# Eight experts for every row, or two: rows scattered into expert order by indirect transfers

## The chip, the cores and the metric

The kernel runs on one core of one Trainium2 chip. The metric is device time in microseconds (us), one launch. A core has TensorE (PE: matrix products into PSUM), VectorE (DVE), ScalarE (ACT), GpSimd (POOL), which can't read PSUM, and SyncE (SP), which issues transfers between the core's SBUF and the chip's memory (DRAM). The engines run their own instruction lists in order and meet at semaphores.

## The reference

A two-layer network over 16 sequences of 256 rows of 128 numbers, 4096 rows in all. Each layer adds (attention) x silu(gated part) to its input. The gated part of the first layer is a mixture of experts, and only its arithmetic matters here:

```
scores = softmax(x @ gate_w.T)                # 8 experts
topw, topi = top_k(scores, 2); topw /= sum(topw)
eo[e]  = (silu(x @ wg[e]) * (x @ wu[e])) @ wd[e]      # each 128 -> 176 -> 128
y      = sum over the two chosen experts of topw * eo
shared = (silu(x @ swg) * (x @ swu)) @ swd            # 128 -> 352 -> 128
g      = silu(y + shared);  x = x + attention * g
```

The reference computes all eight eo for every row and weighs six of them by zero. All numbers are fp32.

## The kernel before

`build_kernel` runs stages one after another, each in a block of its own with a barrier behind it: `front` (layer norm, router logits, loads), `window_attention`, `experts`, then `normalise`, `bias_attention` and `inner_layers` for the second layer. Rows stand in 32 tiles of 128 (X: the running sum, Y: the normalised rows, S: the attention's result).

`window_attention` goes through 64 units (half the heads of a tile at a time; four units make a batch of two tiles). A unit is: scores on PE (L601), a table added and the row maximum on DVE (L701, L705), the maximum taken off on POOL (`shift`, L552), exp on ACT (L676), eight transposes on PE (L609), a copy on ACT (L681), products with the values on PE (L629, L633). POOL also masks the keys of each batch (L546). PE works units off in order; DVE works four units ahead, with six buffers. PSUM bank 7 serves all other small products, in a written order of jobs (JOBS), one at a time. Between units DVE runs `choose_experts` in six parts (two largest of eight scores by maximum and comparison, their weights, and the weights split into three bf16 parts, `wparts`).

`experts` holds all weights side by side as 1760 columns: 1408 routed (8 x 176) and 352 shared, 14 chunks. Each fp32 product is made of three products of rounded and remaining parts (`split_product`, L1118 to L1120). For each of 8 rounds of 512 rows and each chunk, PE makes the gate and the up half (6 products), spreads the rows' weights over the chunk's columns with a 0/1 matrix (L1149), and takes the chunk of two steps before through the down weights (3 products) into one PSUM bank. ACT takes silu and the rounded part (L1208, L1221), DVE multiplies twice (L1258, L1262), POOL makes the remaining part (L1237). A row's weight multiplies its hidden values, so unchosen experts add zero. After 14 chunks ACT takes silu of the sum, PE transposes it, DVE multiplies by S and adds to X (L1265, L1268) and takes statistics (L1272).

```
split_product(ps[0:n, s % 2, :], (wgu_hi[:, 0, a:a + n], wgu_lo[:, 0, a:a + n]), here).then_inc(gate_ps, 1)
...
nc.tensor.matmul(ps[:, 4 + s % 2, :], sel16[:, a:a + n], wT[:, parity, :], start=True, stop=True).then_inc(route_ps, 1)
```

Of the kernel before, what the change touches and what calls it, by code (L numbers as in the profile page):

```python
# [28 lines left out]
RSQRT_MAGIC = 1597463007.0  # L29

# [16 lines left out]
def shape_constants():  # L47
# [19 lines left out]
    select = np.zeros((NE, ROUTED), np.float32)  # L67
    select[np.arange(ROUTED) // INTER, np.arange(ROUTED)] = 1.0
# [6 lines left out]
        "c_select": np.tile(select, (3, 1)),  # L75
# [5 lines left out]
def build_kernel(nc, t, out):  # L81
    ctx = ExitStack()
    with ctx:
# [7 lines left out]
        with ExitStack() as early:  # L91
            S = early.enter_context(nc.sbuf_tensor("S0", [P, NT, P], F32))
            wparts = early.enter_context(nc.sbuf_tensor("wparts", [P, NT, 3 * NE], F32))
            wgu = early.enter_context(nc.sbuf_tensor("wgu", [P, 2, FEAT], F32))
            wd = early.enter_context(nc.sbuf_tensor("wd", [P, len(chunks(FEAT)), P], F32))
            sel = early.enter_context(nc.sbuf_tensor("sel", [3 * NE, ROUTED], F32))
            experts_loaded = early.enter_context(nc.semaphore("experts_loaded"))

            with ExitStack() as first:
# [4 lines left out]
                front(nc, t, ps, X, Y, ident, wgu, wd, sel, experts_loaded, skew, attn, route)  # L104
                window_attention(nc, "a0", t, ps, ident, Y, S, attn, lambda dve, part: choose_experts(nc, dve, part, route, wparts))
            experts(nc, t, ps, ident, X, Y, S, wparts, (wgu, wd, sel, experts_loaded), stats)
# [125 lines left out]

def router_buffers(nc, ctx):

    sb = lambda n, s, d=F32: ctx.enter_context(nc.sbuf_tensor("r_" + n, s, d))
    wide = {n: sb(n, [P, NT, NE]) for n in ("lg", "rest", "first", "second", "wdense")}
    return {**wide, "desc": sb("desc", [P, NE]), "st": sb("st", [P, NT]), "rounded": sb("rounded", [P, NT, NE], BF16)}


def choose_experts(nc, dve, part, route, wparts):  # L240

    lg, rest, first, second, wdense, desc, st, rounded = (route[n] for n in (
        "lg", "rest", "first", "second", "wdense", "desc", "st", "rounded"))
# [3 lines left out]
    def first_of_largest(dst, src):  # L247

        nc.vector.tensor_reduce(st[:, :], src, AX.X, ALU.max)
        dve.drain()  # L250
        nc.vector.tensor_tensor(dst, src, bc(st), ALU.is_equal)
# [8 lines left out]
    if part == 0:  # L260
# [6 lines left out]
        first_of_largest(first[:], lg[:])  # L267
        nc.vector.scalar_tensor_tensor(rest[:], first[:], -2.0, lg[:], ALU.mult, ALU.add)
        dve.drain()
    elif part == 1:  # L270
        first_of_largest(second[:], rest[:])
        nc.vector.tensor_tensor(first[:], first[:], second[:], ALU.add)
        dve.drain()
    elif part == 2:
        nc.vector.tensor_tensor(wdense[:], lg[:], first[:], ALU.mult)
        dve.drain()
        nc.vector.tensor_reduce(st[:, :], wdense[:], AX.X, ALU.add)
# [5 lines left out]
        nc.vector.tensor_tensor(wdense[:], wdense[:], bc(st), ALU.mult)  # L283
        dve.drain()
    else:
        v = part - 3
        kept = wparts[:, :, NE * v:NE * (v + 1)]
        nc.vector.tensor_copy(rounded[:], wdense[:])
        dve.drain()
        nc.vector.tensor_copy(kept, rounded[:])  # L290
        dve.drain()
        if v < 2:
            nc.vector.tensor_tensor(wdense[:], wdense[:], kept, ALU.subtract)
            dve.drain()


def front(nc, t, ps, X, Y, ident, wgu, wd, sel, experts_loaded, skew, attn, route):

    NR, full = ROUTED // P, SHARED // P
    ROUNDS = NT // 4  # L300
    QT = NT // 4
    with ExitStack() as c:
        sb = lambda n, s, d=F32: c.enter_context(nc.sbuf_tensor("r_" + n, s, d))
        sem = lambda n: c.enter_context(nc.semaphore("r_" + n))
# [1867 lines left out]
```

## Time and profile before

| | before |
|---|---|
| runs | 1708.53 us median of 3 (1708.19 to 1713.43) |
| profiled execution | span 1708.8 us, from the first to the last instruction |
| window attention | 30 to 261.6 us |
| experts | 261.6 to 560.0 us |
| PE, DVE, ACT, POOL busy over the span | 89%, 77%, 71%, 64% |

The profile gives one execution. An engine is busy while it runs an instruction; semaphore and register instructions and the issuing of transfers are not counted. A fp32 product of PE shows as two MATMUL records, one of rounded operands and a transpose as one; records overlap, since the engine is pipelined, so the distance between starts says more than a record's length. The granted clock of PE is a share of 2.4 GHz.

### The profile page before, as it was taken

The numbers are of one execution on the slowest core, as the hardware profiler recorded it, in microseconds if no ns is written. First come the engines' busy times: TensorE is split into PE (matmuls) and PEld (weight loads), VectorE is DVE, ScalarE is ACT, GpSimd is POOL, SyncE is SP. The second block draws the span as 40 slices with busy tenths as digits, with TensorE's granted clock in tenths as the row PEclk, the third lists the DMA queues.
The fourth block names the chain that finished last, engine by engine and source line by source line (L and its number), as shares of the span: only waits on it lengthen the run. The fifth ranks groups of instructions, "written<-read, shape, count | busy, mean of one in ns | idle before, by whom it ended". The sixth has DMA issues, their size and how long they took to land. (4 is left out here: it accounts for less than half of the span.)

```text
span 1708.8 us, 44008 instructions
## 1 busy us (share of the span) xinstructions
PE 1513.5 (89%) x16988; PEld 1164.6 (68%) x16988; DVE 1319.0 (77%) x2187; ACT 1217.6 (71%) x2065; POOL 1099.4 (64%) x661
## 2 busy tenths in 40 slices
PE   5899996999999499999999578899999999999885
PEld 4677774677776266666666467777777777777774
DVE  5899974555655699999997788887888888888753
ACT  2677774545445488888888378888888888888873
POOL 1777752555555388888887477776676777667614
PEclk8899998999999699999999689999999999999997
DMA  5000000000000500000000001111111110111113
GB/s 174 2 3 3 3 3 15 15 8 7 7 7 1 185 2 2 14 2 14 2 14 11 13 22 31 27 26 27 27 27 27 27 26 22 26 27 27 27 27 105
DMA packets 56837, 44.12 MB, mean 26 GB/s; under 512 B 28152, under 2 KB 47900, under 8 KB 56388
## 3 DMA queue, kind: packets, MB, share of 16 engines
q1 hardware_dynamic: 56644, 41.45, 9.1%
q8 instruction: 133, 2.18, 0.5%
q14 instruction: 60, 0.49, 0.1%
HBM read 17.75 MB, written 4.23 MB: 13 GB/s over the span
## 5 line engine op out<-in xcount | busy, mean ns | idle before, releaser
L831 POOL TENSOR_TENSOR a_prob<-a_prob,a_top 128x1024 f32<-128x1024 f32 x128 | 239.8, 1895 | 48.2 <-DVE a_top L1023 48.2
L1237 POOL TENSOR_TENSOR e_hh<-e_h,e_hh 128x512 fp32r<-128x512 f32 x112 | 144.8, 1293 | 146.6 <-ACT e_hh L1221 145.2
L1506 POOL TENSOR_TENSOR i_qk<-i_qk,i_rt 128x1024 f32<-128x1024 f32 x64 | 152.0, 2375 | 38.1 <-DVE i_rt L1955 33.3
L1516 POOL TENSOR_TENSOR i_qk<-i_qk,i_rn 128x1024 f32<-128x1024 f32 x64 | 122.5, 1915 | 80.5 <-DVE i_rn L1934 80.5
L1019 DVE TENSOR_TENSOR a_prob<-ps,a_table 128x1024 f32<-128x1024 f32 x128 | 149.7, 1211 | 23.4 <-PE ps L899 21.3
L1811 ACT ACTIVATE i_prob<-i_prob,i_top 128x128 f32<-128x128 f32 x512 | 156.4, 391 | 15.7 <-DVE i_top L1943 13.8
L977 ACT ACTIVATE a_probT<-ps 128x1024 f32<-128x1024 f32 x128 | 131.3, 1026 | 44.5 <-PE ps L907 44.5
L1258 DVE TENSOR_TENSOR e_h<-ps,e_sg 128x512 f32<-128x512 f32 x112 | 77.3, 690 | 104.3 <-PE ps L1120 90.4
L907 PEld LDWEIGHTS ps<-ident,a_prob 128*128 128x128 f32 x1024 | 113.2, 141 | 64.2 <-ACT a_probT L977 50.3
L1503 POOL TENSOR_TENSOR i_qk<-i_raw,i_rot 128x1024 f32<-128x1024 f32 x59 | 140.3, 2378 | 24.1 <-issue 24.1
L1208 ACT ACTIVATE e_sg<-ps 128x512 f32<-128x512 f32 x112 | 67.0, 598 | 123.2 <-PE ps L1120 122.4
L1023 DVE TENSOR_REDUCE a_top<-a_prob 128x4 f32<-128x1024 f32 x128 | 149.5, 1209 | 0.0
L907 PE MATMUL ps<-ident,a_prob 128*128 128x128 f32 x1024 | 138.6, 279 | 5.9 <-ACT a_probT L977 1.3
L552 POOL TENSOR_TENSOR a_prob<-a_prob,a_top 128x1024 f32<-128x1024 f32 x64 | 120.2, 1899 | 28.5 <-DVE a_top L705 28.5
L972 ACT ACTIVATE a_prob<-a_prob 128x1024 f32<-128x1024 f32 x128 | 135.4, 1058 | 0.6 <-POOL a_prob L831 0.6
L1776 ACT ACTIVATE i_raw<-ps 128x1024 f32<-128x1024 f32 x64 | 65.6, 1025 | 76.9 <-PE ps L1573 76.7
L1118 PE MATMUL ps<-e_xT,e_wgu_hi 128*128 128x512 f32 x224 | 89.6, 400 | 4.7 <-DVE e_wd_lo L1284 4.7
L1120 PE MATMUL ps<-e_xT,e_wgu_lo 128*128 128x512 f32 x224 | 89.0, 397 | 0.0
L1119 PE MATMUL ps<-e_xT,e_wgu_hi 128*128 128x512 f32 x224 | 88.7, 396 | 0.0
L1652 PE MATMUL ps<-i_wo,i_oT 128*128 128x128 f32 x512 | 71.8, 285 | 18.6 <-ACT i_oT L1822 18.6
L1955 DVE TENSOR_TENSOR i_rt<-ps,i_rot 128x512 f32<-128x512 f32 x128 | 82.0, 682 | 6.0 <-ACT i_raw L1776 6.0
L1652 PEld LDWEIGHTS ps<-i_wo,i_oT 128*128 128x128 f32 x512 | 65.0, 198 | 28.2 <-ACT i_oT L1822 18.7
(305 smaller groups left out, 4369.3 us busy)
## 6 DMA issues: line engine op xcount, KB each, us to landing
i_V<-i_V SPq DMA_DIRECT2D x96, 130.0 KB, 2.3
a_table<-skew_scratch SPq DMA_DIRECT2D x2, 2048.0 KB, 12.4
X<-in_L_attn_x SPq DMA_DIRECT2D x4, 512.0 KB, 6.1
a_table<-in_c_l_table SPq DMA_DIRECT2D x1, 2048.0 KB, 8.3
e_xs<-Y SPq DMA_DIRECT2D x8, 256.0 KB, 2.3
i_ms<-Y SPq DMA_DIRECT2D x16, 128.0 KB, 2.4
i_ms<-Y SPq DMA_DIRECT2D x16, 112.0 KB, 2.4
out_dram<-X SPq DMA_DIRECT2D x7, 256.0 KB, 2.3
```

What stands on the lines that cost most here:

```text
L831: nc.gpsimd.tensor_tensor(s, s, top[:, slot].unsqueeze(2).broadcast_to([P, HG, KW]), ALU.subtract).then_inc(shifted, 1)
L907: last = nc.tensor.transpose(ps[:, 4 + b // 4, b % 4 * P:(b % 4 + 1) * P], flat[:, b * P:(b + 1) * P], ident[:, :])
L972: nc.scalar.activation(s, s, ACT.Exp).then_inc(exped, 1)
L977: nc.scalar.activation(probT[:, n % 4].rearrange('p (b n) -> p b n', b=2), ps[:, 4:6, :], ACT.Copy).then_inc(pT_sb, 1)
L1019: nc.vector.tensor_tensor(prob[:, slot].rearrange('p (b x) k -> p b x k', b=2), ps[:, 2 * (n % 2):2 * (n % 2) + 2, :].rearrange('p b (x k) ...
L1023: nc.vector.tensor_reduce(top[:, slot], prob[:, slot], AX.X, ALU.max).then_inc(max_done, 1)
L1237: nc.gpsimd.tensor_tensor(hh[0:n, slot(b, parity), 1, :], h[0:n, slot(b, parity), :], hh[0:n, slot(b, parity), 0, :].bitcast(F32), ALU.sub ...
L1503: nc.gpsimd.tensor_tensor(s, raw[:, T % 2], cosines, ALU.mult).then_inc(cos_done, 1)
L1506: nc.gpsimd.tensor_tensor(s, s, rt[:], ALU.add).then_inc(rotated, 1)
L1516: nc.gpsimd.tensor_tensor(flat, flat, rn[:, T // TPB % 2, T % TPB].unsqueeze(2).broadcast_to([P, 2 * FH, FD]), ALU.mult).then_inc(qk_done, 1)
L1652: last = nc.tensor.matmul(ps[:, 3, 0:P], oT[:, u, :], wo[:, layer(T), u, :], start=(u == 0), stop=(u == 3))
L1811: last = nc.scalar.activation(s, s, ACT.Exp, bias=top[:, T % 2, h:h + 1])
```

## The change

`front` loads the routed weights by expert (`wr`, `wd`) and the shared ones apart (`wsh`, `wds`). `choose_experts` keeps each row's two weights and computes where it goes: in each expert's own run of rows, padded to whole blocks of 128 (72 blocks hold 8192 chosen rows and the padding). PE counts with two products (the job `ranks`), DVE adds up the counts. From unit 21 of `window_attention` on, POOL writes the rows into that order in DRAM by 64 indirect transfers (`scatter`: 128 rows of 512 bytes, each to the place in `slot`), two behind each `shift`; SP has written zeros there before. `experts` then has two halves. In the first, 36 pairs of blocks are read back, transposed, taken through one expert's weights, which PE addresses by a number that it loads into a register (`value_load`, 24 at a time), and stored to DRAM (`results`). In the second, the shared expert runs as before, 3 chunks and 8 rounds, while POOL gathers each row's two results by 64 indirect transfers (`fetch`), in between its subtractions (`low`); DVE adds them by weight (`mix`), ACT takes silu, DVE updates X (`renew`).

```diff
 def choose_experts(nc, dve, part, route, place, ranks, ranks_ready, ranks_taken):
...
+        nc.vector.tensor_tensor(rest[:], first[:], second[:], ALU.add).then_inc(route["chosen"], 1)
...
+    elif part == 3:
+        totals, before = ranks[:, 0:NE * NT], ranks[:, NE * NT:2 * NE * NT]
+        dve.wait_ge(*ranks_ready)
+        nc.vector.tensor_tensor_scan(incl[:, :], rank[:, P:P + NE * NT], totals, 0.0, ALU.mult, ALU.add)
...
+    elif part == 4:
...
+            nc.vector.tensor_copy(place["slot"][c][:, :], st[:, :]).then_inc(place["ranked"], 1)
...
+            sp.dma_start(route["rank"][:, :], t["c_rank"]).then_inc(gate_loaded, 16)
...
+            nc.gpsimd.memset(wd[:, :, 1, :], 0.0).then_inc(wd_cleared, 1)
+            nc.gpsimd.memset(route["ones"][:, :], 1.0)
...
 def window_attention(nc, name, t, ps, ident, Y, S, attn, route, place, spent):
...
+    RANKS = 11
+    SCATTERS, PER_UNIT = RANKS + 10, 2
...
+        PARTS = {2: 1, 4: 2, RANKS + 1: 3, RANKS + 3: 4, RANKS + 5: 5}
...
+            sp.wait_ge(zeroed, NZERO)
+            for q in range(NBLOCKS // 4):
+                rows = place["sorted"][4 * P * q:4 * P * (q + 1), :].rearrange("(k p) e -> p k e", p=P)
+                sp.dma_start(rows, place["zeros"][:]).then_inc(place["cleared"], 16)
...
+            nc.gpsimd.memset(place["zeros"][:], 0.0).then_inc(zeroed, 1)
...
+            nc.clear_and_free_semaphores(spent)
+
+            def scatter(r):
+                c, T = divmod(r, NT)
+                if T == 0:
+                    pool.wait_ge(place["ranked"], c + 1)
+                    pool.wait_ge(place["cleared"], 16 * (NBLOCKS // 4))
+                nc.gpsimd.indirect_dma_start(place["sorted"], bass.IndirectOffsetOnAxis(ap=place["slot"][c][:, T:T + 1], axis=0),
+                                             Y[:, T, :], None).then_inc(place["scattered"], 16)
+
             mask_keys(0)
             for n in range(UNITS):
...
                 shift(n)
-                i, r = divmod(n + 2, U)
+                for r in range(PER_UNIT * (n - SCATTERS), PER_UNIT * (n - SCATTERS + 1)):
+                    if 0 <= r < 2 * NT:
+                        scatter(r)
...
+                elif kind == 'ranks':
+                    pe.wait_ge(route["chosen"], 1)
+                    both = route["rest"][:].rearrange("p t e -> p e t")
+                    nc.tensor.matmul(ps[:, 7, 0:NE * NT], route["ones"][:, :], both, start=True, stop=True)
+                    last = nc.tensor.matmul(ps[:, 7, NE * NT:2 * NE * NT], route["rank"][:, 0:P], both, start=True, stop=True)
...
-                if step >= 4 and step % 8 == 4 and step // 8 < 5:
-                    between(dve, 1 + step // 8)
+                if step in PARTS:
+                    choose(PARTS[step])
...
+def experts(nc, t, ps, ident, X, Y, S, place, weights, stats):
...
+            sp.wait_ge(place["scattered"], 16 * 2 * NT)
+            for q in range(QUADS):
+                stage(q)
+                if q >= XBUF - 1:
+                    keep(q - XBUF + 1)
...
+        @block.gpsimd
+        def _(pool):
+            def fetch(i):
+                after(pool, mixed, i - RBUF + 1)
+                for k in range(4):
+                    for ch in range(2):
+                        nc.gpsimd.indirect_dma_start(back[:, i % RBUF, ch, k, :], None, place["results"],
+                                                     bass.IndirectOffsetOnAxis(ap=place["slot"][ch][:, 4 * i + k:4 * i + k + 1], axis=0)).then_inc(returned[i % RBUF], 16)
...
+            for q in range(2):
+                pool.wait_ge(kept[q], 16 * QUADS // 2)
+            fetch(0)
+            for i in range(ROUNDS):
+                if i + 1 < ROUNDS and i + 1 < RBUF:
+                    fetch(i + 1)
+                for s in range(NC):
+                    low(i * NC + s)
+                if RBUF <= i + 1 < ROUNDS:
+                    fetch(i + 1)
...
+            def into(j, owners):
+                pe.wait_ge(rowsT_sb, j // 2 + 1)
+                after(pe, hid_sb, j - 1)
+                for k in range(2):
+                    at = (2 * j + k) % 4 * P
+                    last = nc.tensor.matmul(ps[:, 2 * (j % 2) + k, 0:PAIR], rowsT[:, j // 2 % 2, at:at + P],
+                                            wr[:, bass.ds(owners[k], 1), :, :].rearrange("p a j i -> p (a j i)"), start=True, stop=True)
+                last.then_inc(pair_ps, 1)
...
+            def load_owners(a):
+                for b in range(a, min(a + LOADED, NBLOCKS)):
+                    owners[b] = pe.value_load(place["owner"][0:1, b:b + 1], min_val=0, max_val=NE - 1)
+
+            transpose_rows(0)
+            for j in range(PAIRS + 2):
+                if 2 * j % LOADED == 0 and j < PAIRS:
+                    load_owners(2 * j)
+                if j < PAIRS:
+                    into(j, [owners[2 * j + k] for k in range(2)])
+                if j % 2 == 0 and j // 2 + 1 < QUADS:
+                    transpose_rows(j // 2 + 1)
+                if 0 <= j - 1 < PAIRS:
+                    transpose_hidden(j - 1)
+                if 0 <= j - 2 < PAIRS:
+                    back_out(j - 2, [owners[2 * (j - 2) + k] for k in range(2)])
...
+            def mix(i):
+                dve.wait_ge(out_T, i + 1)
+                dve.wait_ge(returned[i % RBUF], 16 * 8 * (i // RBUF + 1))
...
+                if s == 2 and 0 <= i - 1 < ROUNDS:
+                    mix(i - 1)
+                if s == 1 and 0 <= i - 2 < ROUNDS:
+                    renew(i - 2)
+            renew(ROUNDS - 1)
```

## Rows read from the trace of the kernel before

**Rows 1.** Page, part 1: busy us of each engine (share of the span) xinstructions
```profile
PE 1513.5 (89%) x16988; PEld 1164.6 (68%) x16988; DVE 1319.0 (77%) x2187; ACT 1217.6 (71%) x2065; POOL 1099.4 (64%) x661
```

**Rows 2.** Busy time by stretch: us, busy us (xrecords) of each engine, clock, DMA share, GB/s
```profile
82.00:261.60 179.60, 174.68 (x3812) 130.47 (x3810) 158.06 (x174) 134.09 (x213) 119.90 (x64) 1.00 0.01 3
261.60:276.30 14.70, 2.23 (x8) 1.43 (x8) 6.42 (x4) 8.44 (x7) 1.73 (x2) 0.56 0.15 42
276.30:556.00 279.70, 272.16 (x1180) 197.86 (x1180) 157.04 (x249) 138.67 (x245) 144.78 (x112) 0.99 0.03 7
556.00:560.00 4.00, 0.66 (x5) 0.42 (x4) 2.26 (x6) 0.60 (x1) 0.00 (x0) 1.00 0.00 0
```

**Rows 3.** The same for one batch of the window attention
```profile
216.54:229.48 12.94, 12.85 (x277) 9.54 (x276) 11.52 (x13) 9.98 (x17) 9.36 (x6) 1.00 0.01 3
```

**Rows 4.** Groups by line, experts, 276.3 to 556: busy us, mean ns | idle before
```profile
L1237 POOL TENSOR_TENSOR e_hh<-e_h,e_hh 128x512 fp32r<-128x512 f32 x112 | 144.8, 1293 | 146.6 <-ACT e_hh L1221 145.2
...
L1118 PE MATMUL ps<-e_xT,e_wgu_hi 128*128 128x512 f32 x224 | 89.6, 400 | 4.7 <-DVE e_wd_lo L1284 4.7
...
L1258 DVE TENSOR_TENSOR e_h<-ps,e_sg 128x512 f32<-128x512 f32 x112 | 77.3, 690 | 104.3 <-PE ps L1120 90.4 <-ACT e_sg L1208 13.9
...
L1149 PE MATMUL ps<-e_wT,e_sel 128*128 128x512 bf16 x88 | 34.6, 393 | 0.0
```

**Rows 5.** Waits in the same stretch: us in total, times, longest
```profile
POOL e_hh L1237 <- ACT e_hh L1221: 145.2, 97, 18.5
...
PEld ps L1149 <- issue: 22.4, 81, 0.5
```

**Rows 6.** Timeline of SP's issues behind the experts: start, us
```profile
561.42 0.43 SPq L142 DMA_DIRECT2D a_wnat<-in_L_attn_Wo  x1
```

**Rows 7.** DMA issues by line: KB each, median us to landing
```profile
a_wnat<-in_L_attn_Wo SPq DMA_DIRECT2D x1, 64.0 KB, 1.9
...
e_xs<-Y SPq DMA_DIRECT2D x8, 256.0 KB, 2.3
...
i_ms<-Y SPq DMA_DIRECT2D x32, 0.2 KB, 1.7
```

**Rows 8.** Timeline of PE in the window attention
```profile
150.17 1.13 PE L583 MATMUL ps<-a_xT,a_wT 128*128 128x256 f32 x4
...
154.31 0.27 PEld L629 LDWEIGHTS ps<-a_probT,a_V 128*32 128x32 f32 x16 [0.17 <-issue]
```

**Rows 9.** Timeline of POOL at the start of the window attention
```profile
30.95 0.52 POOL L535 MEMSET a_kM<- 128x512 f32 x1
...
36.09 0.21 POOL L540 MEMSET a_ones<- 128x8 f32 x4
...
36.44 1.89 POOL L546 TENSOR_TENSOR a_kM<-a_kT,a_own 128x1024 f32<-128x1024 f32 x1
```

**Rows 10.** Timeline of DVE: two choosing operations of one size
```profile
96.07 1.22 DVE L275 TENSOR_TENSOR r_wdense<-r_lg,r_first 128x256 f32<-128x256 f32 x1
...
98.54 0.42 DVE L283 TENSOR_TENSOR r_wdense<-r_wdense,r_st 128x256 f32<-128x256 f32 x1
```

**Rows 11.** Chain that ended last, in order of time: start, us, what
```profile
1692.13 2.69 PE ps L1697 x24
```

**Rows 12.** Timeline at the start of the experts
```profile
269.14 0.57 ACT L1192 ACTIVATE e_xT<-ps 128x512 fp32r<-128x512 f32 x1
...
276.34 0.76 PE L1118 MATMUL ps<-e_xT,e_wgu_hi 128*128 128x512 f32 x1 [4.66 <-DVE e_wd_lo L1284]
```

**Rows 13.** Timeline of DVE's statistics: register addresses, then fixed ones
```profile
392.69 0.98 DVE L1272 BATCH_NORM_STATS2 ln_stats<-X  x4 [0.19 <-issue]
...
558.93 0.87 DVE L1272 BATCH_NORM_STATS2 ln_stats<-X 128x6 f32<-128x128 f32 x4
```

**Rows 14.** Timeline of the last round's end
```profile
556.04 0.60 ACT L1203 ACTIVATE e_gT<-ps 128x512 f32<-128x512 f32 x1 [2.64 <-PE ps L1120]
...
557.38 0.69 DVE L1265 TENSOR_TENSOR e_upd<-ps,S 128x512 f32<-128x512 f32 x1 [4.64 <-PE ps L1153]
```

More of the change, by code:

```diff
@@ L233, in router_buffers @@
 def router_buffers(nc, ctx):
     sb = lambda n, s, d=F32: ctx.enter_context(nc.sbuf_tensor("r_" + n, s, d))
[L236 to L243, printed above, removed]
+    wide = {n: sb(n, [P, NT, NE]) for n in ("lg", "rest", "first", "second")}
@@ new lines, in router_buffers, with choose_experts @@
+    return {**wide, "desc": sb("desc", [P, NE]), "rank": sb("rank", [P, P + NE * NT + NBLOCKS]), "ones": sb("ones", [P, P]),
+            "incl": sb("incl", [P, NE * NT]), "dest": sb("dest", [P, NE * NT]), "held": sb("held", [P, NBLOCKS, NE]),
+            "ends": sb("ends", [P, NE]), "need": sb("need", [P, NE]), "st": sb("st", [P, NT]), "count": sb("count", [P, NBLOCKS]),
+            "top": [sb(f"top{c}", [P, NT]) for c in range(2)], "chosen": ctx.enter_context(nc.semaphore("r_chosen"))}
+def choose_experts(nc, dve, part, route, place, ranks, ranks_ready, ranks_taken):
+    lg, rest, first, second, desc, st, rank, incl, dest, held, ends, need, count, top = (route[n] for n in (
+        "lg", "rest", "first", "second", "desc", "st", "rank", "incl", "dest", "held", "ends", "need", "count", "top"))
@@ L289, in choose_experts @@
         dve.drain()
-        nc.vector.tensor_copy(kept, rounded[:])
+        nc.vector.tensor_reduce(count[0:1, :], held[0:1], AX.X, ALU.add)
         dve.drain()
[L292 to L299, printed above, removed]
+        nc.vector.tensor_scalar(count[0:1, :], count[0:1, :], NE - 1.0, None, ALU.min)
@@ L300, in front @@
+        dve.drain()
+        nc.vector.tensor_copy(place["owner"][0:1, :], count[0:1, :])
+        dve.drain()
+def front(nc, t, ps, X, Y, ident, weights, skew, attn, route):
+    full = SHARED // P
     ROUNDS = NT // 4
+    wr, wd, wsh, wds, experts_loaded = weights
     QT = NT // 4
@@ L685, in _ @@
                 for n, kind, i in jobs_at(step):
-                    job(n, kind, i)
+                    if kind != 'ranks':
+                        job(n, kind, i)
                 if 0 <= step < UNITS:
@@ L1095, in after, with quad_of @@
+        staged = [sem(f"staged{q}") for q in range(XBUF)]
+        kept = [sem(f"kept{q}") for q in range(2)]
+        returned = [sem(f"returned{q}") for q in range(RBUF)]
+        block = c.enter_context(nc.Block())
         def after(eng, signal, count):
-            if not isinstance(count, int) or count > 0:
+            if count > 0:
                 eng.wait_ge(signal, count)
+        def quad_of(dram, q):
+            return dram[4 * P * q:4 * P * (q + 1), :].rearrange("(k p) e -> p k e", p=P)
@@ new lines, in renew @@
+            def renew(i):
+                here = slice(4 * i, 4 * i + 4)
+                dve.wait_ge(silu_done, i + 1)
+                nc.vector.tensor_tensor(upd[:], gate[:, i % 2], S[:, here, :], ALU.mult)
+                dve.drain()
+                nc.vector.tensor_tensor(X[:, here, :], X[:, here, :], upd[:], ALU.add)
+                dve.drain()
+                for k in range(4):
+                    nc.vector.bn_stats(stats[:, 4 * i + k, :], X[:, 4 * i + k, :])
+            for j in range(PAIRS + 3):
+                if j < PAIRS:
+                    multiply_pair(j)
+                if j % 2 and j >= 3:
+                    keep_done((j - 3) // 2)
+                if j == 8:
+                    low_weights()
```

511 lines of the change are left out of this document (296 added, 215 removed).

## The prediction, made before the change was run

> **What bounds the kernel now.** The page comes first: TensorE is busy for 89% of the span, GpSimd (POOL) for 64% [rows 1]. A share over the whole span settles nothing, so the stretches come next [rows 2]. The change touches two of them. In the first, the window attention (30 to 261.6 us), one batch of four units takes 12.94 us and PE is busy for 12.85 of them, VectorE (DVE) for 11.52, POOL for 9.36 [rows 3]: PE sets the pace, and POOL has 12.94 - 9.36 = 3.58 us free in each batch. In the second, the experts (261.6 to 560), a start of 14.7 us goes by before the first product, then PE is busy for 272.16 of 279.7 us at full clock with 1180 matmul records, 0.237 us apart, and the last round takes 4 us to drain [rows 2]. The groups by line and the waits say the same from the other side: POOL's 112 subtractions took 144.8 us, and POOL stood idle 145.2 us more for data [rows 4, 5]. So in the experts only PE's record count matters, and everything else is cover.
>
> The stage computes all eight experts for every row: 11 routed and 3 shared chunks of 128 columns, 10 records a routed chunk (9 products and the weight broadcast), 8 rounds of 512 rows. That is 298.4 us from 261.6 to 560.0 [rows 2], and it is the sum that the change takes apart.
>
> **The change, part by part.** Two prices decide it that this trace doesn't show: c, the time for which POOL is held by one indirect transfer (128 rows of 512 B, placed by a list), and v, the time of one register load on PE. Each is bounded first.
>
> For c the nearest row from below is what SP needs to issue a 64 KB load of 128 rows of 512 B, the same shape without a list: 0.43 us [rows 6]. From above it is the whole landing of that load, 1.9 us [rows 7], as if POOL were held until the bytes arrive. An issue is what POOL does here, so I start from the lower row and scale it by the engine: the same 128x512 work takes 1.293 us on POOL and 0.690 on DVE [rows 4], a factor of 1.9, though one of those reads PSUM. 0.43 x 1.9 is 0.8; with the list to read first I take c = 0.86. The range keeps 0.43 and 1.9.
>
> The Trainium skill (DMA: Bandwidth & Descriptors, Latency and other measured facts) puts the first byte of a transfer from GpSimd at about 1 us, because GpSimd's own cores write the descriptors, against about 0.6 us from SP. No run here shows a POOL transfer; SP's 0.43 us doesn't contradict it [rows 6]. If all of that 1 us held POOL, the sum below would end near 1697, an estimate that lies inside the forecast's own range.
>
> For v: from below, PE's sequencer issues 16 weight loads in 0.27 us, 0.02 each [rows 8]; from above, the smallest DMA of the trace lands in 1.7 us [rows 7]; the nearest is the gap of 22.4 / 81 = 0.28 us that PE has where its sequencer works out a wait from a loop register [rows 5]. I take 0.28.
>
> *Router and front.* One more 228 KB load (SP, about 0.43 us) and two memsets fall into slack at the start. In the attention POOL's memsets run straight into its first key mask (36.09, then 36.44, no wait) [rows 9], so the added 128x512 memset is on the path: 0.52 us by its twin, plus the semaphore clears, about 1 us together. The ranks job adds two fp32 products of 256 columns on the engine that sets the pace: one pair takes 1.13 us [rows 8]. The choosing parts change from some 15 small DVE operations to some 25, most 0.2 to 0.42 us: about 8.5 us as before, but three parts fall into two batches, where DVE has 1.4 us free each [rows 3, 10]; one such row took 1.22 instead of 0.42 us beside POOL [rows 10]. I put 2 us on it. Together +4 us. The 18 clearing writes go from SP, which has nothing else there.
>
> *Scatters.* 64 issues, two behind each of 32 shifts, so 8 batches hold 8 each. POOL then needs 9.36 + 8c a batch against 12.94. Below c = 0.45 all is hidden behind PE. Above it each batch is late by 8c - 3.58, and what is queued behind an issue is the next unit's shift, then its exponential and its transposes. Sum: 64c - 28.6, at 0.86 **+26.4 us**.
>
> *Routed experts.* 36 pairs of blocks. PE per pair, in fp32: 12 products in a row at 128 columns took 2.69 us, 0.224 each [rows 11], so two of 352 columns take 352/128 x 0.224 x 2 = 1.23, four of 128 take 0.90; six transposes (four hidden, two rows), one record each where a product has two, take half of 0.224 each, 0.67. That is 2.80; with two cross-engine hops a pair that don't fully overlap, 2.95. ScalarE has 0.60 + 0.30 + 0.41 us and DVE about 0.8 a pair (512 columns: 0.57 to 0.69 us [rows 4, 12]), so PE still sets the pace, and POOL idles. 36 x 2.95 = 106. Six operands a pair are addressed by register: on DVE four such operations took 0.98 us against 0.87 with fixed addresses [rows 13], 0.03 each; I count none, since PE's sequencer runs ahead, and 6 us as the bound. The 72 register loads come in bursts of 24: the first is in the start, the other two stop PE for 24 x 0.28 = 6.7 each, less about 0.7 of queued work: 12. Start: SP issues at once (0.5), the rows land after 2.3 [rows 7], then 6.7 of loads, then the first product: 10.4 against 14.7, since the weights are split later, under the pairs. Drain of the last pair, its copy and its store: 6.5.
>
> *Shared expert and return.* PE has 27 products a round at 0.237, and 8 transposes: 7.3 us. POOL has 8 gathers and 3 subtractions of 1.293: 3.9 + 8c, which is 10.8 at 0.86. So POOL sets the pace there from c = 0.43 on. The first 16 gathers stand ahead of the first subtraction, and PE waits for that. A gather also waits until the round two before it is mixed: subtraction 1.3, product 0.8, transposes 0.7, mixing 2.3 come to 5.1, with four hops 5.5, against the 3.9 that the three subtractions cover, 1.6 late in six rounds. Sum: 64c + 31 + 10. The tail is longer than today's by the mixing: 7 against 4 [rows 2, 14].
>
> Experts: 10.4 + 106 + 12 + 6.5 + 31 + 10 + 7 + 64c = 183 + 64c, at 0.86 **238 us** against 298.4: -60.
>
> *Sum.* -60 + 26.4 + 4 = -30 us. The profiled execution spans 1708.8 us, 0.3 above the median of the runs, so the runs should show **1679 us**. In c alone: 1708.8 + 128c - 140, which crosses zero at c = 1.09.
>
> **Rivals.**
> - *POOL is too slow (slower).* One mechanism: an indirect issue holds POOL for over 1.09 us. Both added sets then cost more than the products save. At c = 1.4 the scatters add 61 us, the experts need 273, and the time is 1748; at 1.9 it is 1812. For it: 1.9 us is a real row, and POOL is the slower engine on like work [rows 4, 7]. Against it: 0.43 us for the like issue on SP [rows 6]. Chance 0.34.
> - *The issues are nearly free.* At c of 0.45 or less the attention hides every scatter and PE sets the pace of the shared expert; 183 + 28 = 211, and the time is about 1626. For it: the SP row. Against it: a list must be read. Chance, up to c = 0.6: 0.17.
> - *Register loads stop PE.* They stand in PE's own order, with nothing behind them to run. At v = 1.7 the three bursts cost 122 us instead of 20: 1679 + 102 = 1781. For it: nothing on PE overlaps them, and the smallest transfer takes 1.7 [rows 7]. Against it: no transfer may be needed. Doubling v to 0.6 moves the time to 1702. Chance that they alone turn the sign: 0.05.
> - The Trainium skill (the same page and section) gives a register load from memory a floor of about 600 ns; by that the sum would end near 1702, inside the forecast's own range, so it has no chance apart. The trace before has no such load on PE that could agree or not.
> - *No gain from fewer products.* If the pairs ran at the round trip through ScalarE and DVE and not at PE's 2.80, each would take some 4 us, 38 us more: 1717. PE works two pairs ahead, so I leave it inside the last 0.06, with no change.
>
> **How the numbers follow.** This measurement can tell about 0.3% (5 us) from no change; the three runs span 5 us. The forecast, c from 0.6 to 1.05, has 0.38; its own range is 1645 to 1710. Faster: 0.38 + 0.17 = 0.55. Slower: 0.34 + 0.05 = 0.39. Same: 0.06. The range that leaves out 2 in 10 runs from the free issues (1626) to c = 1.55 (1767): 1625 to 1768. The bounds alone (c = 1.9, v = 1.7) would reach beyond it, and I leave them out.
>
> **What the profile after would show.** Right: POOL rows for indirect transfers of 0.6 to 1.05 us; attention batches of 14 to 18 us where scatters run and 12.9 elsewhere; 36 pairs about 3 us apart; three holes of some 7 us in PE; rounds of the shared expert of 10 to 13 us with POOL full; the bias attention and all behind it unmoved. Wrong, if the indirect rows exceed 1.1 us or POOL waits between them for descriptors; if PE's holes at the register loads exceed 15 us; or if PE's half clock in the emptier second half (the granted clock was 0.56 in the experts' start, and the first 512-column record took 0.76 us instead of 0.40) [rows 2, 4, 12] makes a round longer than POOL's.

## The result, and where the time went

The changed kernel takes 1868.35 us (median of 4 runs, 1864.05 to 1876.21) against 1708.38 us: a ratio of 1.0908, 95% interval 1.0882 to 1.0934. It is slower by 9%, outside the forecast range and on the other side of its sign. The profiled execution spans 1862.3 us; the forecast, put on the same footing, was 1678.8, so 183.5 us have to be found. The page of the kernel after, part 1, and of part 2 PE's busy tenths and its granted clock in 40 slices:

```profile
PE 1471.8 (79%) x16728; PEld 1145.3 (61%) x16728; DVE 1251.8 (67%) x2141; ACT 1154.9 (62%) x1978; POOL 1109.4 (60%) x702
...
PE   6878879556565553999999976889999999999985
...
PEclk7888889787788685999999977999999999999998
```

PE is busy for 42 us less than before [rows 1], and the span is 154 us longer: the products went, and waits came. Slices 8 to 16 (326 to 745 us) are the experts, where PE falls to half busy; its granted clock is 0.79 and 0.75 there, against 0.88 in the attention ahead of them, which lost less. The busy time by stretch (us, busy us of each engine with its records, clock, DMA share, GB/s):

```profile
0.00:41.60 41.60, 27.74 (x123) 24.19 (x123) 19.40 (x78) 11.80 (x25) 8.11 (x19) 0.75 0.63 181
41.60:339.50 297.90, 236.59 (x4383) 172.66 (x4382) 203.33 (x223) 159.13 (x253) 213.47 (x144) 0.88 0.11 32
339.50:562.60 223.10, 128.27 (x648) 101.07 (x648) 31.05 (x57) 45.76 (x94) 0.00 (x0) 0.79 0.15 42
562.60:713.50 150.90, 74.05 (x280) 55.76 (x280) 57.38 (x143) 39.54 (x72) 92.06 (x88) 0.75 0.11 30
713.50:1862.30 1148.80, 1005.15 (x11295) 791.59 (x11295) 940.62 (x1642) 898.67 (x1534) 795.77 (x452) 0.95 0.11 29
```

The first key mask of POOL begins the second stretch, SP's first load of sorted rows the third, the shared expert's first transposes the fourth; the fifth is set as long as what lay behind 560.0 us before [rows 2]. It holds the same work at the same pace: from the bias attention's first key mask to the end are 1130.8 us, and 1131.5 before. Against the prediction's terms (times in us):

| stretch | predicted | measured | off |
|---|---|---|---|
| to the first key mask | 36.4 + 1 | 41.6 | +4 |
| choosing and ranks (first to 7th mask; 76.5 before) | 76.5 + 3 | 96.8 | +17 |
| scatters (7th to 16th mask; 116.5 before) | 116.5 + 26.4 | 168.5 | +26 |
| routed pairs, start and drain | 10.4 + 106 + 12 + 6.5 | 223.1 | +88 |
| shared expert, gathers, tail | 55 + 31 + 10 + 7 | 150.9 | +48 |

**The pairs.** PE's groups by line from SP's first load of rows to the first gather (busy us, mean ns | idle before), then the timeline of one burst and one quad of rows:

```profile
L1253 PE MATMUL ps<-wr,e_rowsT 128*128 x144 | 58.2, 533 | 43.3 <-issue 43.3
...
L1245 PE MATMUL ps<-ident,e_rows 128*128 128x128 f32 x72 | 16.6, 372 | 50.4 <-DMA e_rows<-sorted_scratch 50.4
```

```profile
427.04 2.71 PE L1253 MATMUL ps<-wr,e_rowsT 128*128 x4 [14.17 <-issue]
...
431.80 1.35 PE L1253 MATMUL ps<-wr,e_rowsT 128*128 x4
...
434.32 1.35 PE L1253 MATMUL ps<-wr,e_rowsT 128*128 x4
...
435.75 0.36 SPq L1193 DMA_DIRECT2D results_scratch<-e_done  x1
436.16 0.51 SPq L1189 DMA_DIRECT2D e_rows<-sorted_scratch  x1
439.11 0.65 PE L1245 MATMUL ps<-ident,e_rows 128*128 128x128 f32 x4 [3.45 <-DMA e_rows<-sorted_scratch]
```

Three things stand here. The hole (idle stretch) of 14 us ahead of the first row is the burst of 24 register loads, 0.6 us each; the four records behind it take 2.71 us where the same four take 1.35 a pair later: the granted clock is 0.50 there, from 427 to 430 us. Then the pairs come 2.52 us apart (2.74 on average, with the transposes of the rows), faster than the 2.95 that I forecast. And the last three rows are the new wait: PE has nothing else from 435.66 us on; SP issues the load of the next rows at 436.16, right behind the store of an earlier quad (four blocks, two pairs), and the rows land 3.0 us later. So the load comes 0.5 us too late to hide any of its landing, and not 2.5 us ahead, as experiment 1's expectation has it. PE waits for rows 14 times, 50.4 us; the first time, 3.6 us, is the start.

**The scatters.** POOL's timeline over one batch:

```profile
273.29 1.91 POOL L617 TENSOR_TENSOR a_kM<-a_kT,a_own 128x1024 f32<-128x1024 f32 x1
275.14 1.91 POOL L623 TENSOR_TENSOR a_prob<-a_prob,a_top 128x1024 f32<-128x1024 f32 x1
277.21 1.01 POOL L637 DMA_INDIRECT sorted_scratch<-Y,p_slot  x1 [0.17 <-issue]
278.52 0.96 POOL L637 DMA_INDIRECT sorted_scratch<-Y,p_slot  x1 [0.30 <-issue]
...
292.54 1.90 POOL L617 TENSOR_TENSOR a_kM<-a_kT,a_own 128x1024 f32<-128x1024 f32 x1
```

A batch takes 19.25 us instead of 12.94 [rows 3], and POOL has no idle time but the 0.17 and 0.30 us ahead of each transfer, which no row counts as busy. Its five other operations take 1.9 us each, so one scatter costs (19.25 - 9.5) / 8 = 1.22 us: c, which I took as 0.86.

**The shared half.** One round of it, POOL with what its third subtraction waits for:

```profile
676.30 0.67 DVE L1454 TENSOR_TENSOR e_h<-ps,e_sg 96x512 f32<-96x512 f32 x1
...
680.87 0.94 POOL L1213 DMA_INDIRECT e_back<-results_scratch,p_slot  x1 [0.31 <-issue]
681.83 2.50 POOL L1220 TENSOR_TENSOR e_hh<-e_h,e_hh 128x512 fp32r<-128x512 f32 x2
683.15 0.80 PE L1237 MATMUL ps<-e_hh,e_wds_hi 128*128 128x512 f32 x1 [8.35 <-POOL e_hh L1220]
...
686.86 0.60 ACT L1381 ACTIVATE e_sg<-ps 128x512 f32<-128x512 f32 x1 [11.51 <-PE ps L1239]
...
687.35 0.62 ACT L1387 ACTIVATE e_hh<-e_h 96x512 fp32r<-96x512 f32 x1
...
688.04 1.29 POOL L1220 TENSOR_TENSOR e_hh<-e_h,e_hh 96x512 fp32r<-96x512 f32 x1 [3.72 <-ACT e_hh L1387]
689.48 0.96 POOL L1213 DMA_INDIRECT e_back<-results_scratch,p_slot  x1
```

Eight gathers 1.25 us apart (10 us), then two subtractions, then a wait of 3.7 us for the third chunk's data, then the third; a round takes some 17.5 us, against the 10 to 13 forecast. The third chunk (96 rows) is not late at PE or DVE: DVE has multiplied it at 676.3. What is late is its rounded part, at 687.35 on ACT. In ACT's order that stands behind the silu of the next round's first chunk; PE makes that chunk only behind the product that waits for the first subtraction (8.35 us), and the first subtraction is queued behind the gathers.

### The profile page after: what moved, and what is told of

It reads as the page before. It is cut to its first block and busy times, and to the rows that moved or that the text cites. A ratio compares the mean times of both kernels' runs of the same rounds, so it can differ in the third digit from the quotient of the medians.

```text
span 1862.3 us, 43144 instructions
## 1 busy us (share of the span) xinstructions
PE 1471.8 (79%) x16728; PEld 1145.3 (61%) x16728; DVE 1251.8 (67%) x2141; ACT 1154.9 (62%) x1978; POOL 1109.4 (60%) x702
## 5 line engine op out<-in xcount | busy, mean ns | idle before, releaser
L1213 POOL DMA_INDIRECT e_back<-results_scratch,p_slot x64 | 61.7, 964 | 258.1 <-DMA results_scratch<-e_done 239.6
L1112 DVE TENSOR_TENSOR a_prob<-ps,a_table 128x1024 f32<-128x1024 f32 x128 | 149.6, 1210 | 23.3 <-PE ps L992 21.2
L1429 DVE TENSOR_TENSOR e_hid<-ps,e_act_g 128x352 f32<-128x352 f32 x36 | 18.9, 524 | 190.7 <-ACT e_act_g L1365 190.7
L1065 ACT ACTIVATE a_prob<-a_prob 128x1024 f32<-128x1024 f32 x128 | 135.5, 1058 | 0.6 <-POOL a_prob L924 0.6
L1370 ACT ACTIVATE e_hidT<-ps 128x512 f32<-128x512 f32 x36 | 21.5, 597 | 154.6 <-PE ps L1263 154.6
L765 ACT ACTIVATE a_prob<-a_prob 128x1024 f32<-128x1024 f32 x64 | 67.4, 1054 | 63.2 <-POOL a_prob L623 62.5
L794 DVE TENSOR_TENSOR a_prob<-ps,a_table 128x1024 f32<-128x1024 f32 x64 | 75.2, 1216 | 44.2 <-PE ps L690 44.0
L1253 PE MATMUL ps<-wr,e_rowsT 128*128 x144 | 58.2, 533 | 43.3 <-issue 43.3
L2155 DVE TENSOR_REDUCE i_top<-i_prob 128x8 f32<-128x1024 f32 x64 | 78.1, 1220 | 6.1
```

The source lines that it names most:

```text
L1065: nc.scalar.activation(s, s, ACT.Exp).then_inc(exped, 1)
L1112: nc.vector.tensor_tensor(prob[:, slot].rearrange('p (b x) k -> p b x k', b=2), ps[:, 2 * (n % 2):2 * (n % 2) + 2, :].rearrange('p b (x k) ...
```

## The experiments

Stretches below are read from each run's trace: "pairs" from SP's first load of rows to the first gather (226.0 us in the kernel after), "return" from there to the next attention's first key mask (165.9). My theory after the profile: four separate losses, SP's order, register loads, POOL's price for a transfer, and POOL's queue in the shared half. The rivals stand in the expectations. Experiments 1 to 10 are one run each, and the four runs of the kernel after lie 12 us apart, so a gain is read from the stretches that its edit touches, and not from the time alone.

**1. The order on SP.**

```diff
-                if q >= XBUF - 1:
-                    keep(q - XBUF + 1)
+                if q >= XBUF + 1:
+                    keep(q - XBUF - 1)
```

> Edit: on SP, the load of a quad of sorted rows is no longer queued behind the store of the quad three before it, but behind that of the quad five before it. Theory A (the rows are late because SP's order holds their load back until the store is issued, 2.5 us before PE wants rows that take 3.0 us to land): PE's 14 waits for the rows, 50.4 us, go almost to nothing, and with them part of the half-clock work behind each wait. The pair phase falls from 223 to 160 to 175 us, the whole from 1868 to 1805 to 1820. Rival B (the waits only cover another limit, such as the round trip through ScalarE and VectorE, so that a pair can't be faster): the pair phase falls by less than 15 us.

1796.1 us; span 1794.3, so 68.0 less; the pairs fall to 158.3. PE's wait for rows, over the whole pairs, is 3.6 us in all, at the start; below it the pairs by stretch, in the kernel after and then here (us, busy us of each engine with its records, clock, DMA share, GB/s):

```profile
L1245 PE MATMUL ps<-ident,e_rows 128*128 128x128 f32 x72 | 12.4, 301 | 3.6 <-DMA e_rows<-sorted_scratch 3.6
```

```profile
339.52:565.53 226.01, 129.74 (x656) 102.19 (x657) 31.74 (x58) 46.35 (x95) 0.00 (x0) 0.80 0.15 42
```

```profile
340.88:499.20 158.32, 107.88 (x656) 86.97 (x657) 31.77 (x58) 46.37 (x95) 0.00 (x0) 0.84 0.22 61
```

Theory A holds, and its bound was too small: 47 us of waits gone gave 68. The rest is clock: the granted clock of the pairs rose from 0.80 to 0.84 and PE needed 108 busy us for the work that took it 130.

**2. One instruction for 24 register loads.**

```diff
-                for b in range(a, min(a + LOADED, NBLOCKS)):
-                    owners[b] = pe.value_load(place["owner"][0:1, b:b + 1], ...)
+                _, values = nc.values_load_multi_w_load_instructions(place["owner"][0:1, a:a + LOADED], ...)
```

> Edit: the 24 register loads of a burst are one instruction that loads 24 registers. Theory A (each register load holds PE's sequencer for 0.6 us, 14.4 of the 15 us hole at each of the three bursts): the holes shrink to 2 to 6 us, and the whole falls by 27 to 39 us to 1830 to 1841. Rival B (the hole is something else that stands at the same place, a wait for weights or code): the holes stay at 15 us and the time at 1868.

1844.74 us; span 19.4 less. The second burst's hole, in PE's timeline:

```profile
414.15 2.71 PE L1253 MATMUL ps<-wr,e_rowsT 128*128 x4 [6.97 <-issue]
```

The hole follows the number of load instructions, so it is the loads; but a register still costs 7.0 / 24 = 0.29 us, and both the hole and the gain miss what I expected (2 to 6 us, and 27 to 39).

**3. The subtraction on DVE.** POOL's `low(g)` becomes DVE's, behind the multiplication of the next chunk.

```diff
-                nc.gpsimd.tensor_tensor(hh[0:n, g % HBUF, 1, :], h[...], hh[...], ALU.subtract)
+                nc.vector.tensor_tensor(hh[0:n, g % HBUF, 1, :], h[...], hh[...], ALU.subtract)
```

> Edit: the subtraction of the high part in the shared expert goes from POOL to DVE; POOL keeps the gathers alone. Theory A (PE stands in the product of the way back for a subtraction that is queued behind 8 gathers, then the next chunk's round trip runs with POOL idle, so gathers and round trip add up): the shared half falls from 151 us to the gathers' own 64 x 1.25 = 80 plus 10 to 16 of start and tail, so by 50 to 60 us; the whole is 1805 to 1820, and POOL's indirect rows follow each other 1.25 us apart. Rival B (the gathers themselves set the pace and the subtractions cost only their 31 us): it falls by 31 us, to 1837. Rival C (DVE becomes the limit, with 3 more operations of 0.69 us a round): it falls by less than 31 us.

1816.9 us; the return falls from 165.9 to 109.5, by 56.4, and POOL issues gather upon gather. The span fell by 47.3 only, since stretches that the edit doesn't touch were 9 us longer in this run (the pairs by 4.6, what lies behind by 3.1, the choosing by 2.7, the scatters shorter by 1.3). Theory A: the 31 us of subtractions that left POOL don't explain 56 alone, some 25 more are the chain, and DVE was not the limit.

**4. No scatters.** SP copies the rows in their own order.

```diff
+            for r in range(2 * NT):
+                sp.dma_start(place["sorted"][P * r:P * (r + 1), :], Y[:, r % NT, :]).then_inc(place["scattered"], 16)
...
-                        scatter(r)
```

> Leaves out: the sorting. 64 plain copies by SP put the rows of Y into the sorted buffer in their own order, POOL scatters nothing. Theory A (each scatter holds POOL for 1.22 us, 0.97 shown and 0.25 between, so that a batch with 8 of them needs 9.4 + 9.8 us of POOL instead of PE's 12.94): the batches come back to 12.94 us, the stretch from the 7th to the 16th key mask falls from 168.5 to 117, and the whole by about 52 us to 1816. Rival B (the batches are long because PE runs at half clock behind its holes, or because the 18 clearing writes and the choosing disturb it): they stay above 15 us.

1822.02 us; span 42.1 less, as the pairs were 5.4 us longer in this run and other stretches 4. Two key masks of POOL:

```profile
206.17 1.89 POOL L620 TENSOR_TENSOR a_kM<-a_kT,a_own 128x1024 f32<-128x1024 f32 x1 [2.58 <-ACT a_kT L752]
...
219.11 1.89 POOL L620 TENSOR_TENSOR a_kM<-a_kT,a_own 128x1024 f32<-128x1024 f32 x1 [2.58 <-ACT a_kT L752]
```

They are 12.94 us apart, as before the change, and the 7th to the 16th mask take 117.1 instead of 168.5. All 52 us of the scatters are POOL's, none the clearing writes'. The choosing stayed at 98.5.

**5. Owners known at build time.** On top of experiment 1.

```diff
-                    owners[b] = pe.value_load(place["owner"][0:1, b:b + 1], ...)
+                    owners[b] = NE * b // NBLOCKS
...
-                                            wr[:, bass.ds(owners[k], 1), :, :]
+                                            wr[:, owners[k]:owners[k] + 1, :, :]
```

> Leaves out: the routing of the weights. Block b takes the expert number 8b/72 rounded down, known when the kernel is built, so that PE loads no register and its weights have fixed addresses; the rows come early, as in e1_rows_ahead, with which it is compared (pair phase there 158.3 us from SP's first load of rows to the first gather, pairs 2.52 us apart). Theory A (the loads cost 0.6 us each and an operand that is addressed by register costs nothing beside them): the three holes of 14.8 us go, the pairs stay 2.52 us apart, and the stretch falls by 40 to 46 us to 112 to 118. Rival B (the address by register also costs PE): the pairs come closer than 2.4 us and the stretch falls by more than 50.

1749.23 us; the pairs take 110.27, so 48.0 less than in experiment 1, 2 more than theory A's bound and less than rival B's 50. What tells the two apart is the distance of the pairs. Two pairs in PE's timeline:

```profile
362.09 1.35 PE L1253 MATMUL ps<-wr,e_rowsT 128*128 128x352 f32 x4
363.28 0.60 PE L1263 MATMUL ps<-ident,e_hid 128*128 128x128 f32 x4
363.71 1.06 PE L1273 MATMUL ps<-wd,e_hidT 128*128 128x128 f32 x8
364.61 1.35 PE L1253 MATMUL ps<-wr,e_rowsT 128*128 128x352 f32 x4
365.79 0.60 PE L1245 MATMUL ps<-ident,e_rows 128*128 128x128 f32 x4
...
367.56 1.35 PE L1253 MATMUL ps<-wr,e_rowsT 128*128 128x352 f32 x4
```

Two pairs with one set of rows take 5.47 us; in experiment 1, with registers, SP's stores of a quad are as far apart:

```profile
426.69 0.36 SPq L1193 DMA_DIRECT2D results_scratch<-e_done  x1
...
432.16 0.36 SPq L1193 DMA_DIRECT2D results_scratch<-e_done  x1
```

So an operand that is addressed by register costs PE nothing here; the loads cost 48 us, 44 in their holes and the rest in the half-clock records behind them.

**6. The first three together.**

> The edits of e1_rows_ahead, e2_grouped_loads and e3_low_dve together. If the three losses are independent, their gains add up: 68 + 20 + 47 to 1868 - 135 = 1733 us, with the stretch from the first load of rows to the first gather near 137 us and from there to the next attention's first key mask near 110. If one hides another (the rows hide behind the register loads, say), the sum falls short by 10 us or more.

1731.19 us; span 133.2 less than the kernel after, where the three gains add to 68.0 + 19.4 + 47.3 = 134.7; the pairs take 140.3 us (137 expected), the return 110.8. The losses are independent within these few us.

**7. The ranks taken at once.** On top of 6.

```diff
-        PARTS = {2: 1, 4: 2, RANKS + 1: 3, RANKS + 3: 4, RANKS + 5: 5}
+        PARTS = {2: 1, 4: 2, RANKS: 3, RANKS + 3: 4, RANKS + 5: 5}
```

> As e6_three, and DVE takes the ranks from PSUM one step earlier, ahead of the next pair of score additions and maxima instead of behind them. Theory A (PE's next product for the attention waits for the PSUM bank that holds the ranks, which DVE empties 8 us after they are there, and that hole of 6.5 us drains the pipeline): the hole falls to 1 to 3 us and the stretch from the 4th to the 7th key mask (59 us for three batches of 12.94 = 39) gets 4 to 9 us shorter. Rival B (DVE's own added work sets that stretch): it changes by less than 2 us.

1719.74 us. PE's product that follows the ranks into the same PSUM bank, in the kernel after and then here:

```profile
107.58 2.07 PE L677 MATMUL ps<-a_wT,a_xT 128*128 128x128 f32 x8 [6.50 <-DVE r_dest L310]
```

```profile
105.73 1.16 PE L677 MATMUL ps<-a_wT,a_xT 128*128 128x128 f32 x8 [1.99 <-DVE r_dest L310]
```

The hole is 6.50 us in experiment 6 too. The 4th to the 7th mask take 49.6 us instead of 62.2 there, the first to the 7th 91.5 instead of 100.5. Theory A holds for the hole. How much the stretch gained is less sure: the first to the 7th mask take 96.8 to 101.5 us in the eight traces that have the hole (96.8 in the kernel after), 91.5 here and 93.9 in experiment 8, so between 3 and 10 us.

**8. One scatter behind each shift.** On top of 7; the last 21 follow the last shift.

```diff
-    SCATTERS, PER_UNIT = RANKS + 10, 2
+    SCATTERS, PER_UNIT = RANKS + 10, 1
...
+            for r in range(PER_UNIT * (UNITS - SCATTERS), 2 * NT):
+                scatter(r)
```

> As e7_ranks_soon, with one scatter behind each shift instead of two; the last 21 stand behind the last shift. Theory A (POOL's sum sets the batch: 9.5 + 1.22 for each scatter): 10.7 batches of 14.4 us instead of 8 of 19.25, 16 us lost instead of 52, and of the last 21 scatters (26 us) some 13 lie beside the drain of the attention and 13 behind it; it ends 20 to 26 us earlier than e7_ranks_soon. Rival B (a scatter costs the attention what it costs wherever it stands): the same time within 5 us.

1704.29 us. Batches of 14.21 us, by two key masks of POOL:

```profile
235.26 1.90 POOL L617 TENSOR_TENSOR a_kM<-a_kT,a_own 128x1024 f32<-128x1024 f32 x1
...
249.46 1.91 POOL L617 TENSOR_TENSOR a_kM<-a_kT,a_own 128x1024 f32<-128x1024 f32 x1
```

SP's first load of rows comes at 319.1 instead of 335.2 us: 16 earlier, less than the 20 to 26 expected. The batches were as forecast, but from the 16th mask to that load it is 55.5 us instead of 32.6: 23 us of trailing scatters lie behind the attention, where I had allowed 13.

**9. Gathers of 64 rows.** As 6, with half the rows in each gather.

```diff
-  back[:, i % RBUF, ch, k, :], ... place["slot"][ch][:, 4 * i + k:4 * i + k + 1]
+  back[0:64, i % RBUF, ch, k, :], ... place["slot"][ch][0:64, 4 * i + k:4 * i + k + 1]
```

> Leaves out: half of the gathered rows. As e6_three, but each of the 64 gathers takes 64 rows instead of 128 (the other half of the buffer is zero). Theory A (the 1.25 us from one indirect transfer to the next is paid per row that POOL writes down, beside a small fixed part): the row of 0.94 us falls to 0.5 to 0.6 us and the distance to 0.8 to 0.9; the stretch from the first gather to the next attention's first key mask, 110.8 us in e6_three, falls by 20 to 28. Rival B (a fixed price of the instruction): the row stays above 0.85 us and the stretch within 6 us.

1724.31 us, the return 110.25 against 110.77. Durations of the 64 gathers (min/median/max ns), in experiment 6 and then here:

```profile
L1213 POOL DMA_INDIRECT e_back<-results_scratch,p_slot x64: 940/945/1596, 483.4 to 568.3; - x64
```

```profile
L1213 POOL DMA_INDIRECT e_back<-results_scratch,p_slot x64: 893/904/1823, 479.3 to 563.9; - x64
```

0.90 us for 64 rows, where the median is 0.945 for 128: rival B. For a gather the price is the instruction's, not the rows'; scatters were not tried. The Trainium skill (DMA: Bandwidth & Descriptors, Anatomy of one DMA — SWDGE (gpsimd) path) says of writing descriptors that "You can emit a lot of descriptors before the incremental cost shows up"; the trace agrees, 64 more rows cost 0.04 us.

**10 to 12. What is left.** Experiment 10 takes 8, moves PE's loads for 48 blocks ahead of its wait for the rows, and the ranks one batch earlier (`RANKS = 7`):

```diff
+            load_owners(0)
+            load_owners(LOADED)
             transpose_rows(0)
```

11 adds the key mask by ScalarE and 5 scatters a batch:

```diff
-                    nc.scalar.activation(kT[:, :], k, ACT.Copy).then_inc(k_sb, 1)
+                    for x in range(QG):
+                        last = nc.scalar.activation(kM[:, par, x, PAD:PAD + SEQ], k, ACT.Copy, scale=own[:, x:x + 1])
+                    last.then_inc(masked, 1)
```

12 moves those loads to the end of PE's program for the attention.

> As e8_one_per_unit, with the register loads of the first 48 blocks ahead of PE's wait for the sorted rows, where PE has nothing to do, and the ranks, the slots and the scatters 4 units (one batch) earlier. Expected: the first hole of 8 us in the pairs goes and the second too, some 14 us, and 4 scatters less stand behind the attention, 5 us: 1704 - 19 = 1685 us. If PE's holes were hiding something else, less than 8 us comes.

> As e10_early, with the key mask written by ScalarE straight from PSUM (four copies scaled by the mask's columns) instead of by POOL, and 5 scatters a batch. POOL then needs 7.6 + 5 x 1.22 = 13.7 us a batch against 9.5 + 4 x 1.22 = 14.4: batches of 13.5 to 13.8 us instead of 14.2, and 11 scatters less behind the attention. Expected 15 to 20 us below e10_early: 1665 to 1670 us, faster than the kernel before. If ScalarE's 1.1 us more a batch lies on the attention's own chain, batches stay above 14 us and only the 11 scatters (13 us) are won.

> As e11_best, with the first 48 register loads at the end of PE's work for the attention instead of at the start of its work for the experts. Theory A (in e10_early and e11_best PE could not load early, since no engine starts on the experts until POOL has issued its last scatter, so 15 us of loads still stood between the landing of the rows and the first product): PE loads while POOL scatters, the first products follow the rows, and the time falls by 11 to 15 us to 1656 to 1660. Rival B (what stands there is the transfer of the rows or the weights, not the loads): the time stays at 1671.

10: 1698.52 us, a gain of 6 where I expected 19: PE's last product of the attention ends at 298.4 us, but SP's and ScalarE's first instructions of the experts stand at 316.2, behind POOL's last scatter (to 310.6), and PE's loads hold its first transposes until 333.7. 11: 1671.38 us (1667.14 to 1674.85, 4 runs), a ratio to the kernel before (1714.46 us, 7 runs taken with it) of 0.9745, interval 0.9719 to 0.9772: this version is faster than the kernel before and the kernel after. It lies 27 us below 10, where I expected 15 to 20; its batches take 13.6 to 13.8 us, as expected. 12: 1672.91 us, ratio 0.9752 (0.9728 to 0.9777), so no gain. SP's first load and PE's first transposes, in 11 and then in 12:

```profile
293.24 19.09 SPq L1187 DMA_DIRECT2D e_rows<-sorted_scratch  x4
...
310.83 1.11 PE L1235 MATMUL ps<-ident,e_rows 128*128 128x128 f32 x4 [20.77 <-issue]
```

```profile
308.17 8.82 SPq L1192 DMA_DIRECT2D e_rows<-sorted_scratch  x5
...
311.18 1.08 PE L1240 MATMUL ps<-ident,e_rows 128*128 128x128 f32 x4 [20.26 <-DMA e_rows<-sorted_scratch]
```

In 11 the rows are asked for at 293 and PE's loads hold it until 310.8. In 12 PE loads first, and SP asks for the rows at 308, where ScalarE's first instruction of the experts stands too (308.19): by these starts, no engine begins the experts before all have ended the attention. The 15 us moved from behind the stage's border to ahead of it. Theory A of 12 is wrong, and so is its rival: it is the loads, but PE has no idle time there to do them in. Its last product of the attention ends at 290.9 us, POOL's last scatter at 288.6.

## Why the prediction was wrong

**The step that failed first: "Routed experts ... SP issues at once (0.5), the rows land after 2.3".** I followed the rows to the first product and no further. The sum has no term for the rows of the other 17 quads, and I did not walk SP's order, in which each load is queued behind a store that waits for DVE, so that 13 of them went out 0.5 us or more after PE had come to need the rows. Experiment 1: 68.0 us, by itself enough to turn -30 into a loss. With the terms below, 68 + 29 + 50 + 23 + 17 + 4, less 8 for pairs that were faster than forecast, comes to 183 of the 183.5 us. Of PE's own work the step was right, with margin: 2.74 us a pair against the 2.95 taken (98 against 106 us), and registers as addresses cost nothing.

**v, one register load on PE.** Taken 0.28, measured 0.6 (a hole of 14.17 for 24, a little work hidden). The loads cost 48 us against some 19 in the sum, 29 more. The rival at 0.6 was priced at 23 more, near enough; the mechanism was right, the size wrong. The row I took as the nearest was a wait worked out from a loop register, which turned out to be another thing. The Trainium skill's figure (DMA: Bandwidth & Descriptors, Latency and other measured facts), about 600 ns, was the better number; the trace agrees with it, at 14.17 / 24 = 0.59.

**c, the time that POOL is held.** Taken 0.86, measured 1.22 to 1.25. The row alone (0.94 to 0.98) was close; the 0.17 to 0.30 us between rows was not foreseen, and what fills it is not shown. c lies beyond the break-even of 1.09, so the first rival, that POOL is too slow, came true as well: with c = 1.24 the sum gives 1708.8 + 158.7 - 140 = 1727.5, a loss, without any of the other errors. It explains some 50 of the 183.5 us: 26 in the attention, where 64c - 28.6 at 1.22 gives 49.5 and 52.0 were measured, and 25 in the gathers. That the row came near 0.86 was luck: I had scaled an issue by the speed of elementwise work, and experiment 9 shows a price that hardly depends on the rows.

**Shared expert: "5.5, against the 3.9 that the three subtractions cover".** The gathers' own 25 us apart, 23 of the 48 us here are a chain that I had closed too early. I let PE wait for a subtraction but not what stands behind PE's wait in its own order: the next chunk's product, with it ScalarE's silu, and behind that, in ScalarE's order, the rounding that the third subtraction waits for. Experiment 3 takes the subtractions (31 us) and that chain (25) off POOL's queue and gives 56 us.

**Choosing: "I put 2 us on it".** Measured 20.3 with the ranks, against 3. DVE's choosing operations there sum to 18.7 us, not 8.5, as six of them take 1 to 2 us. Two of them, beside POOL's subtractions for the attention (three, the last to 126.00):

```profile
120.39 5.61 POOL L623 TENSOR_TENSOR a_prob<-a_prob,a_top 128x1024 f32<-128x1024 f32 x3
...
122.39 1.78 DVE L322 TENSOR_SCALAR r_need<-r_need 128x8 f32<-128x8 f32 x1
124.24 2.03 DVE L324 TENSOR_TENSOR r_dest<-r_dest,r_need 128x256 f32<-128x256 f32 x1
```

Each of the six began while such a subtraction of 1.9 us ran and ended 0.03 to 0.61 us behind its end, and so did the row of 1.22 us before the change [rows 10], at 97.29 against 97.01. That row was the warning, and I took its neighbour of 0.42 as the rule. By these ends the long operations waited for POOL's; no run tests it, and others (L269, L275, L308) ran beside such a subtraction in 0.41 to 0.42. Another 3 to 10 us was the PSUM bank of experiment 7: I priced the two products and not the hold on the bank that PE needs next. The 15 to 17 us that remain in experiments 7 and 8 are more than the rows leave: 18.7 us on DVE against the 1.4 us that it has free in each of six batches [rows 3], and 2.1 us of ranks' products on PE, come to 12.4. That is worked out, not tried, and the rest stays open.

**The first 41.6 us.** PE's clock there was granted at 0.50 from 22 to 31 us, against 0.64 before and 0.92 in experiment 5, whose first mask came at 35.3. The attention's own start, from its first memset to the first mask, took 6.5 us in both, against 5.6 before, so the +1 was right. The rest is the front, which ended late where the clock was low. Of the thirteen traces with the changed front twelve show 0.50 or 0.51 there; why, and whether the change brings it about, is not shown.

**Right:** everything behind the experts unmoved; PE's order of work in the pairs and its price; POOL as the limit where scatters run, and where gathers run once the chain is cut. Of the signs that I had named, the three holes at the loads came, 14 to 15 us each instead of 7, and the indirect rows (medians 0.94 and 0.97 us) lay within 0.6 to 1.05, while the distance between them did not. The attention's batches (19.25 us, 14 to 18 forecast) and the shared expert's rounds (17.5, 10 to 13) did not come as forecast. The free-issue rival is out, and so is the round trip as the pairs' limit.

## What to carry to other kernels

When work is replaced by data that arrives on demand, walk the issuing queue through a steady-state period, not only through the start: write down what stands ahead of each load, when that is released, and how long the bytes take; here 13 of the 18 loads needed 3.0 us and went out 0.5 us or more after their rows were wanted. When an engine waits, list what is queued behind it in its own order and who waits for that, until the list closes: a subtraction behind eight gathers stopped PE, and through PE's and then ScalarE's own order it held back the third subtraction. And a small transfer or register load that is issued some 64 times is a stage of its own: price it from start to start, the gap included.

## What was not expected of the hardware

- A gather by indirect transfer holds POOL for 0.90 us with 64 rows and 0.945 with 128 (medians), and the next starts 0.30 us later.
- 24 register loads in one instruction take 7.0 to 8.0 us, 24 single ones 14.2 to 15.
- The loss through the clock is a large addition to a wait: 47 us of waits removed gave 68, as records behind a hole ran at half speed (2.71 us for four at a granted clock of 0.50, where 1.35 is usual) and the mean granted clock of the stretch rose from 0.80 to 0.84 without them.
- On DVE one operation of 128x256 took 0.42 us and another 2.03, and an operation of 8 elements a partition 1.78 us: the long ones ended right behind a subtraction of POOL's during which they had begun.
